# Unscaled scores on VectorE and the inverse root in the exponentials of ScalarE, for the last four narrow jobs

## The chip, the cores and the metric

The kernel runs on one core of a Trainium2 chip. The metric is the device time of one execution in microseconds, lower is better. Before the change the median of three runs was 381.04 us (380.89 to 381.19).

## The reference

Four cross-attention layers run one after another on `x` (8 batches x 128 tokens x 128 channels) against a context of 8 x 128 x 256. Layers 0 and 3 are narrow: 16 query heads of width 8 over 4 key/value heads, with an RMS norm of the input. Layers 1 and 2 are wide: 16 heads of width 64 and a bias on a few key columns. Cut to what matters:

```python
def narrow(x, cond, wq, wk, wv, wo, norm_w):                  # layers 0 and 3
    inv = rsqrt(mean(x * x, axis=-1) + 1e-5)                  # one number per token
    q = (x * inv * norm_w) @ wq;  k = cond @ wk;  v = cond @ wv
    scores = einsum('btgrd,bsgd->bgrts', q, k) / sqrt(8)
    attn = softmax(scores)                                    # over the 128 keys
    return x + einsum('bgrts,bsgd->btgrd', attn, v) @ wo
def wide(x, cond, Wq, Wk, Wv, Wo, bo):                        # layers 1 and 2
    return softmax(q @ k.T / 8 + col_bias) @ v @ Wo + bo + x
x = narrow(wide(wide(narrow(x, L0), L1), L2), L3)
```

The inverse root `inv` is one factor per token (per row of scores), so it may be applied to the scores in place of the input.

## The kernel before, in words

A job is one layer for one batch, 32 jobs in all. They are ordered in two turns of 16: the first turn does all four layers for batches 0 to 3, the second for batches 4 to 7. The last four jobs, n = 28 to 31, are therefore layer 3, narrow, for batches 4 to 7. A job has two halves, o = 2n and 2n + 1, and a half has two sides; one side is a score tile of 128 tokens x 512 (four heads x 128 keys), in one PSUM bank. The last four jobs are halves 56 to 63.

The order of work on every engine is written out by hand in that engine's `half` function, and every engine takes its instructions strictly in that order, with semaphores between engines. Nothing is planned at run time. A side goes through these steps:

- TensorE, `scores` (L825 narrow, L836 wide): the scores, with sign reversed by the factor put on the queries.
- VectorE, `scores_out` (L615): four instructions of 128x128, one for each head. Each copies negated scores from PSUM to `probs`, adds a bias (`no_bias`, a column of zeros that is broadcast, in narrow jobs), multiplies by `scale`, and accumulates the minimum over keys to `negmax`. In narrow jobs `scale` is the per-token column `inv_rms`, read from memory; in wide jobs it is the constant 1.0. A short read of the accumulator follows each.
- ScalarE, `exponentials` (L482): four activations of 128x128, exp(-1.0 * e + negmax), in place, each with its row sum and a read of the accumulator. The scale is a constant and the bias a column.
- VectorE, `inverse_sums` (L622): reciprocal of the row sums. GpSimd, `normalise` (L379): multiplies probabilities by it.
- TensorE, `transpose_probs` (L849), two halves later. The transposed tile is copied out (`probsT`) by VectorE for side 0 (L626) and, in halves whose own job is narrow, by ScalarE for side 1 (L499). That copy stands between the exponentials of side 0 and side 1 of the half two later.
- TensorE, weighted values (L870 narrow, L882 wide), VectorE `oT` (L631, L633), TensorE output projection (L900), VectorE adds the input (L641, L643), and a DMA stores the batch after layer 3 (L310).

VectorE's order within half o is: add the input of job n - 2 and write the mean square (L586) if o is odd; `scores_out(o, 0)`; `inverse_sums(o - 1, 1)`; `scores_out(o, 1)`; `oT`; if o is even, the two instructions that make the next job's queries (L594, L598); copies of the transposes of half o - 2; `inverse_sums(o, 0)`. ScalarE's order in the last halves is: exponentials of side 0, the copy L499, exponentials of side 1.

The inverse root of job n is made by GpSimd (`inverse_root`, L361) in its half 2n - 2, from the mean that VectorE wrote; VectorE waits for it before the first scores of the job.

Of the kernel before, what the change touches and what calls it, by code (L numbers as in the profile page):

```python
# [27 lines left out]
ALU = mybir.AluOpType  # L28
ACT = mybir.ActivationFunctionType
# [4 lines left out]
P = 128  # L34
# [15 lines left out]
NARROW = (0, 3)  # L50
# [23 lines left out]
NJOBS = len(JOBS)  # L74
NARROW_JOBS = [n for n, (l, b) in enumerate(JOBS) if l in NARROW]
WIDE_ROWS = [(p, l) for p, l in ROWS if l not in NARROW]
NARROW_ROWS = [(p, l) for p, l in ROWS if l in NARROW]
KV_RING = 3
KD_RING = 2
# [33 lines left out]
def job(n):  # L113

    return JOBS[n] if 0 <= n < NJOBS else (None, None)
# [12 lines left out]
def uses(n, h):  # L128

    return sum(2 if is_wide(m) else 1 for m in range(n)) + (h + 1 if is_wide(n) else 1)  # L130


def scores_bank(o):

    return "fill" if o >= LAST_FILL + 2 and o % 2 == 1 else "scores"
# [12 lines left out]
def narrow_index(n):  # L148

    return NARROW_JOBS.index(n)  # L150


def build(nc, xT, ctxT, narrow_w, narrow_kv, kv_w, qo_w, small, tokens, outT):
    with ExitStack() as ctx:
        def sb(name, shape, dt=F32):
            return ctx.enter_context(nc.sbuf_tensor(name, shape, dt))

        def sem(name):
            return ctx.enter_context(nc.semaphore(name))
# [38 lines left out]
        x_sq = sb("x_sq", [P, 2, T])  # L198
        rms = sb("rms", [P, 2])
        inv_rms = sb("inv_rms", [P, 2])  # L200
        c_hi = sb("c_hi", [P, PAIRS, CC, PAIR], F32R)
        c_lo = sb("c_lo", [P, PAIRS, CC, PAIR], F32R)
        kT = sb("kT", [P, KV_RING, IC, PAIR])
# [13 lines left out]
        negmax = sb("negmax", [P, 2, 2, 4])  # L217
# [32 lines left out]
        sq_ready, rms_out, rms_made = sem("sq_ready"), sem("rms_out"), sem("rms_made")  # L250
# [6 lines left out]
        pt_full, pt_read = pair("pt_full"), pair("pt_read")  # L257
        v_full, v_read = sem("v_full"), sem("v_read")
        y_full, y_read = sem("y_full"), sem("y_read")
        out_stored = sem("out_stored")  # L260

        HALVES = [(n, h) for n in range(NJOBS + 2) for h in range(2)]
# [51 lines left out]
        def _(pool):  # L314
# [43 lines left out]
            def inverse_root(n):  # L358

                pool.wait_ge(rms_out, narrow_index(n) + 1)  # L360
                nc.gpsimd.tensor_tensor(inv_rms[:, n % 2:n % 2 + 1], rms[:, n % 2:n % 2 + 1], half_power[:],  # L361
                                        ALU.pow).then_inc(rms_made, 1)

            def square(n):

                l, b = job(n)
                if l == 0:
                    pool.wait_ge(x_loaded[0 if b < 2 else 1], 16)
                else:
                    pool.wait_ge(y_read, JOBS.index((2, b)) + 1)  # L370
                if narrow_index(n) >= 2:
                    pool.wait_ge(ms_full, narrow_index(n) - 1)
                nc.gpsimd.tensor_tensor(x_sq[:, n % 2, :], x[:, b, :], x[:, b, :], ALU.mult).then_inc(sq_ready, 1)
# [19 lines left out]
            def half(o):  # L393
                if valid(o):
                    normalise(o, 0)
                    normalise(o, 1)
                for n in NARROW_JOBS:
                    if o == 2 * n - 2 and n > 0:
                        inverse_root(n)
                    if o == 2 * n - 4 and n >= 2:  # L400
                        square(n)
                    if o == keys_half(n):
                        if job(n)[1] % 2 == 0:
                            split_keys(f"kn{job(n)[1] // 2}.{job(n)[0]}")
                        diagonal_keys(n)
                    if o == 2 * n:
                        narrow_values(n)
                if o in (3, 4):
                    split_piece(o + 1)
                if o == 9:  # L410
                    split_context(2)
                if o == 10:
                    split_context(3)
# [6 lines left out]
            pool.wait_ge(smalls_loaded, 16)  # L420
            diagonal_keys(0)
            inverse_root(0)
            square(1)
            diagonal_keys(1)
# [5 lines left out]
        def _(act):  # L430
# [46 lines left out]
            def exponentials(o, side):  # L477

                act.wait_ge(scores_read[side], o + 1)
                for q in range(4):  # L480
                    e = probs[:, o % PROBS_RING, side, q * S:(q + 1) * S]
                    last = nc.scalar.activation(e, e, ACT.Exp, scale=-1.0, bias=negmax[:, o % 2, side, q:q + 1],  # L482
                                                accum_out=rowsum[:, o % 2, side, q:q + 1])
                last.then_inc(exps_made[side], 1)

            def half(n, h):
                o = 2 * n + h
                if h == 0 and is_wide(n):
                    wide_queries(n, 1)
                if h == 1 and is_wide(n + 1):  # L490
                    wide_queries(n + 1, 0)
                for name in FILLS.get(o - 1, [])[1:]:
                    if name != "bias":
                        fill_out(name)
                if valid(o):
                    exponentials(o, 0)
                if scalar_copy(o - 2):
                    act.wait_ge(pt_full[1], o - 1)
                    nc.scalar.activation(probsT[:, (o - 2) % PROBST_RING, 1, :], pt_ps[1][:], ACT.Copy).then_inc(pt_read[1], 1)  # L499
                if valid(o):  # L500
                    exponentials(o, 1)
                for name in FILLS.get(o, [])[:1]:
                    fill_out(name)
                if o in (0, 1):
                    round_piece(o + 2)
                if 3 <= o <= 6:
                    round_piece(o + 1)
# [18 lines left out]
        def _(dve):  # L526
# [77 lines left out]
            def scores_out(o, side):  # L604

                n, h = o // 2, o % 2
                l, b = job(n)
                bias = no_bias[:].broadcast_to([P, S]) if l in NARROW else col_bias[:, l - 1, :]
                scale = inv_rms[:, n % 2:n % 2 + 1] if l in NARROW else 1.0
                if l in NARROW and h == 0 and side == 0:  # L610
                    dve.wait_ge(rms_made, narrow_index(n) + 1)
                dve.wait_ge(scores_full[side], o + 1)
                for q in range(4):
                    cols = slice(q * S, (q + 1) * S)
                    last = nc.vector.tensor_tensor_reduce(  # L615
                        out=probs[:, o % PROBS_RING, side, cols], in0=banks[scores_bank(o)][side][:, cols], in1=bias, scale=scale,
                        scalar=HUGE, op0=ALU.add, op1=ALU.min, accum_out=negmax[:, o % 2, side, q:q + 1])
                last.then_inc(scores_read[side], 1)
# [28 lines left out]
            def half(n, h):  # L647
# [5 lines left out]
                if valid(o):  # L653
                    scores_out(o, 0)
                if valid(o - 1):
                    inverse_sums(o - 1, 1)
                if valid(o):
                    scores_out(o, 1)
# [38 lines left out]
        def _(pe):  # L697
# [14 lines left out]
            def context_split(p):  # L712
                if p == 0:
                    pe.wait_ge(c_split, 1)
                else:
                    pe.wait_ge(rest_split, p)
# [7 lines left out]
            def project_context(name):  # L724
# [29 lines left out]
                else:  # L754
                    f, m = int(name[1]), int(name[3])
                    p, l = WIDE_ROWS[f]
                    context_split(p)
# [51 lines left out]
            def scores(n, h):  # L809
# [18 lines left out]
                pe.wait_ge(q_read, uses(n, h))  # L828
                f = WIDE_ROWS.index((b // 2, l))
                for m in (2 * h, 2 * h + 1):  # L830
# [21 lines left out]
            def weighted_values(n, h):  # L852
# [12 lines left out]
                if l in NARROW:  # L865
# [9 lines left out]
                    return  # L875
                f = WIDE_ROWS.index((b // 2, l))
                name = f"v{f}.{2 * (b % 2) + h}"
# [123 lines left out]
```

## Time and profile before

| | us |
|---|---|
| median of three runs | 381.04 |
| the profiled execution, its own time | 380.89 |
| its span (first to last instruction) | 379.1 |
| outside the span | 1.79 |
| busy PE / DVE / ACT / POOL | 359.7 / 267.7 / 279.0 / 187.6 |

Half 56 starts on VectorE at 333.98 us, the last exponential ends at 371.46 us, and the span ends at 379.1 us. Each half can be found by its first exponential of ScalarE, at 335.19 us for half 56, 341.28 for 57, 345.37 for 58, 351.01 for 59, 354.58 for 60 and 359.87 for 61. PE is TensorE's matmuls, PEld its weight loads, DVE VectorE, ACT ScalarE, POOL GpSimd, SP the engine that issues the stores. Busy time overlaps a little between neighbouring instructions of one engine, because each starts before the last has quite ended: a mean duration is not always the distance from start to start.

### The profile page before, as it was taken

To read this page: it belongs to the slowest core of one execution; us is meant where nothing else is said; L and a number is where in the kernel's file an instruction comes from. 1 tells how busy PE (TensorE), PEld (TensorE's weight loads), DVE (VectorE), ACT (ScalarE), POOL (GpSimd) and SP (SyncE) were. 2 spreads that over 40 slices of the span, in tenths; PEclk is the share of its full clock that TensorE was granted. 3 is DMA by queue.
4 is the path that set the end of the run, shared out by engine and by line. 5 is a ranking of instruction groups with operands and counts; after the bars stand their busy time and mean duration, and the time that the engine had idled before them with its cause. 6 is when DMAs were issued, how large, how long until landed. Compare 5 with 4: busy or idle time off the path is not lost.

```text
span 379.1 us, 10494 instructions
## 1 busy us (share of the span) xinstructions
PE 359.7 (95%) x3522; PEld 319.1 (84%) x3522; DVE 267.7 (71%) x1401; ACT 279.0 (74%) x1176; POOL 187.6 (49%) x220
## 2 busy tenths in 40 slices
PE   8889999999999999999999999999999999978665
PEld 8787799899999998889889988888999989867554
DVE  2999975636536547696978886577564785699982
ACT  4889998865665567475899999998566865647793
POOL 3677853733223236454676765443333435447662
PEclk9899999999999999999999999999999999999979
DMA  7925000000000000000000000000000000000000
GB/s 232 411 66 216 1 3 3 2 3 2 1 2 3 2 0 3 2 3 0 10 3 9 9 8 2 3 3 2 0 3 2 3 2 1 2 3 3 7 9 14
DMA packets 4883, 9.91 MB, mean 26 GB/s; under 512 B 608, under 2 KB 3296, under 8 KB 4576
## 3 DMA queue, kind: packets, MB, share of 16 engines
q1 hardware_dynamic: 4400, 8.91, 6.5%
q8 instruction: 29, 0.48, 0.5%
q10 hardware_dynamic: 432, 0.34, 0.4%
q14 instruction: 22, 0.18, 0.2%
HBM read 8.73 MB, written 0.52 MB: 24 GB/s over the span
## 4 chain that ended last, share of the span: by engine, by line
PE 74%; DVE 21%; ACT 3%; issue 1%; DVEq 0%; POOL 0%; POOLq 0%
PE pt_ps L849 13%; PE scores_ps L836 9%; DVE probs L615 8%; PE q_ps L796 8%; PE fill_ps L701 7%; PE v_ps L900 7%; PE v_ps L882 7%; PE fill_ps L702 7%; PE fill_ps L703 7%; PE v_ps L870 3%; DVE probsT L626 3%; ACT probs L482 3%; PE q_ps L788 2%; DVE qn L598 2%; DVE qn L594 2%; PE scores_ps L825 2%
## 5 line engine op out<-in xcount | busy, mean ns | idle before, releaser
L482 ACT ACTIVATE probs<-probs,negmax 128x128 f32<-128x128 f32 x512 | 198.5, 391 | 81.0 <-DVE negmax L615 80.9
L379 POOL TENSOR_TENSOR probs<-probs,inv 128x512 f32<-128x512 f32 x128 | 137.3, 1075 | 176.8 <-DVE inv L622 176.4
L482 ACT ACTIVATION_READ_ACCUMULATOR probs<-probs,negmax 128x1 f32 x512 | 96.8, 189 | 0.0
L615 DVE CUSTOM_DVE_ANT_0 probs<-scores_ps,col_bias 128x128 f32<-128x128 f32 x256 | 58.2, 284 | 39.1 <-PE scores_ps L836 39.1
L849 PE MATMUL pt_ps<-smalls,probs 128*128 128x128 f32 x512 | 70.5, 282 | 6.2 <-DVE probsT L626 6.2
L849 PEld LDWEIGHTS pt_ps<-smalls,probs 128*128 128x128 f32 x512 | 57.6, 143 | 18.2 <-issue 14.8
L615 DVE CUSTOM_DVE_ANT_0 probs<-scores_ps,no_bias,inv_rms 128x128 f32<-128x128 f32 x224 | 64.2, 343 | 5.8 <-PE scores_ps L825 5.4
L626 DVE COPY probsT<-pt_ps 128x512 f32<-128x512 f32 x96 | 63.0, 684 | 2.6 <-PE pt_ps L849 0.5
L615 DVE DVE_READ_ACCUMULATOR2_ANT negmax<- 128x1 f32 x512 | 42.5, 83 | 0.0
L701 PE MATMUL fill_ps<-c_hi,w_hi 128*128 128x256 f32 x128 | 38.3, 300 | 0.0
L836 PE MATMUL scores_ps<-kT,qT 64*128 64x128 f32 x512 | 37.2, 285 | 0.0
L882 PE MATMUL v_ps<-probsT,v 128*64 128x128 f32 x512 | 35.0, 279 | 1.6 <-DVE rms L586 1.0
L702 PE MATMUL fill_ps<-c_hi,w_lo 128*128 128x256 f32 x128 | 36.1, 282 | 0.0
L703 PE MATMUL fill_ps<-c_lo,w_hi 128*128 128x256 f32 x128 | 36.0, 281 | 0.0
L836 PEld LDWEIGHTS scores_ps<-kT,qT 64*128 64x128 f32 x512 | 31.1, 187 | 3.9
L796 PE MATMUL q_ps<-x,w_qo 128*128 128x128 f32 x256 | 34.0, 276 | 0.0
L882 PEld LDWEIGHTS v_ps<-probsT,v 128*64 128x64 f32 x512 | 27.4, 136 | 7.1 <-issue 4.0
L796 PEld LDWEIGHTS q_ps<-x,w_qo 128*128 128x128 f32 x256 | 31.9, 191 | 1.3 <-issue 0.4
L900 PE MATMUL v_ps<-oT,w_qo 128*128 128x128 f32 x256 | 31.7, 277 | 0.0
L643 DVE SCALAR_TENSOR_TENSOR x<-v_ps,smalls,x 128x128 f32<-128x128 f32 x16 | 5.6, 347 | 35.3 <-PE v_ps L900 35.3
L900 PEld LDWEIGHTS v_ps<-oT,w_qo 128*128 128x128 f32 x256 | 29.9, 192 | 0.0
L701 PE MATMUL fill_ps<-w_hi,c_hi 128*128 128x512 f32 x64 | 27.5, 430 | 0.3 <-ACT v L468 0.3
(92 smaller groups left out, 583.2 us busy)
## 6 DMA issues: line engine op xcount, KB each, us to landing
kT<-in_kv_w SPq DMA_DIRECT2D x6, 512.0 KB, 6.4
w_qo<-in_qo_w SPq DMA_DIRECT2D x2, 1024.0 KB, 8.3
v<-in_ctxT SPq DMA_DIRECT2D x4, 256.0 KB, 9.5
v<-in_kv_w SPq DMA_DIRECT2D x2, 512.0 KB, 11.2
outT<-x SPq DMA_DIRECT2D x8, 64.0 KB, 1.6
wn<-in_narrow_w SPq DMA_DIRECT2D x2, 192.0 KB, 5.7
x<-in_xT SPq DMA_DIRECT2D x1, 384.0 KB, 8.1
oT<-in_narrow_kv ACTq DMA_DIRECT2D x1, 256.0 KB, 3.9
```

The costliest lines, as they stand in the source:

```text
L379: nc.gpsimd.tensor_tensor(p4, p4, inv[:, o % 2, side, :].unsqueeze(2).broadcast_to([P, 4, S]), ALU.mult,).then_inc(probs_made[side], 1)
L482: last = nc.scalar.activation(e, e, ACT.Exp, scale=-1.0, bias=negmax[:, o % 2, side, q:q + 1], accum_out=rowsum[:, o % 2, side, q:q + 1])
L615: last = nc.vector.tensor_tensor_reduce(out=probs[:, o % PROBS_RING, side, cols], in0=banks[scores_bank(o)][side][:, cols], in1=bias, scal ...
L626: nc.vector.tensor_copy(probsT[:, o % PROBST_RING, side, :], pt_ps[side][:]).then_inc(pt_read[side], 1)
L701: nc.tensor.matmul(out, a_hi, b_hi, start=(n == 0), stop=False)
L702: nc.tensor.matmul(out, a_lo, b_hi, start=False, stop=False)
L703: last = nc.tensor.matmul(out, a_hi, b_lo, start=False, stop=(n == len(moving) - 1))
L796: last = nc.tensor.matmul(q_ps[:, c * T:(c + 1) * T], w_qo[:, l - 1, first:first + P], x[:, b, :], start=True, stop=True)
L836: last = nc.tensor.matmul(out[side][:, c * S:(c + 1) * S], qT[rows, 4 * h + c, :], kT[rows, f % KV_RING, 4 * h + c, b % 2 * S:(b % 2 + 1) ...
L849: last = nc.tensor.transpose(pt_ps[side][:, cols], probs[:, o % PROBS_RING, side, cols], identity)
L882: last = nc.tensor.matmul(v_ps[side * WIDE_D:(side + 1) * WIDE_D, c * T:(c + 1) * T], v[:, f % KV_RING, b % 2, head * WIDE_D:(head + 1) * ...
L900: last = nc.tensor.matmul(y_ps, w, oT[:, c, :], start=(c == 0), stop=(c == (1 if l in NARROW else IC) - 1))
```

## The change

In jobs 28 to 31 (`n >= LATE`) VectorE no longer multiplies the scores by `inv_rms`. Its `scale` is the constant 1.0, as in wide jobs, it still adds the broadcast column of zeros, and it no longer waits for the inverse root. ScalarE makes `shift = inv_rms * negmax` (an activation of 128x4, one per side) and then takes exp(neg_rms * e + shift), with `neg_rms` and `shift` as columns. ScalarE waits for its own write of `shift` and for `neg_rms`, which GpSimd makes by one more instruction of 128x1 for each job, right behind the inverse root and after a wait for it.

```diff
--- before.py
+++ after.py
@@ -74,6 +74,8 @@
 NJOBS = len(JOBS)
 NARROW_JOBS = [n for n, (l, b) in enumerate(JOBS) if l in NARROW]
 WIDE_ROWS = [(p, l) for p, l in ROWS if l not in NARROW]
+
+LATE = NJOBS - 4
 NARROW_ROWS = [(p, l) for p, l in ROWS if l in NARROW]
 KV_RING = 3
 KD_RING = 2
@@ -198,6 +200,8 @@
         x_sq = sb("x_sq", [P, 2, T])
         rms = sb("rms", [P, 2])
         inv_rms = sb("inv_rms", [P, 2])
+        neg_rms = sb("neg_rms", [P, 2])
+        shift = sb("shift", [P, 2, 2, 4])
         c_hi = sb("c_hi", [P, PAIRS, CC, PAIR], F32R)
         c_lo = sb("c_lo", [P, PAIRS, CC, PAIR], F32R)
         kT = sb("kT", [P, KV_RING, IC, PAIR])
@@ -257,6 +261,7 @@
         pt_full, pt_read = pair("pt_full"), pair("pt_read")
         v_full, v_read = sem("v_full"), sem("v_read")
         y_full, y_read = sem("y_full"), sem("y_read")
+        neg_made, shift_made = sem("neg_made"), sem("shift_made")
         out_stored = sem("out_stored")
 
         HALVES = [(n, h) for n in range(NJOBS + 2) for h in range(2)]
@@ -360,6 +365,10 @@
                 pool.wait_ge(rms_out, narrow_index(n) + 1)
                 nc.gpsimd.tensor_tensor(inv_rms[:, n % 2:n % 2 + 1], rms[:, n % 2:n % 2 + 1], half_power[:],
                                         ALU.pow).then_inc(rms_made, 1)
+                if n >= LATE:
+                    pool.wait_ge(rms_made, narrow_index(n) + 1)
+                    nc.gpsimd.tensor_scalar(neg_rms[:, n % 2:n % 2 + 1], inv_rms[:, n % 2:n % 2 + 1], -1.0, None,
+                                            ALU.mult).then_inc(neg_made, 1)
 
             def square(n):
 
@@ -477,9 +486,17 @@
             def exponentials(o, side):
 
                 act.wait_ge(scores_read[side], o + 1)
+                n = o // 2
+                offset, scale = negmax, -1.0
+                if n >= LATE:
+                    act.wait_ge(neg_made, n - LATE + 1)
+                    nc.scalar.activation(shift[:, o % 2, side, :], negmax[:, o % 2, side, :], ACT.Copy,
+                                         scale=inv_rms[:, n % 2:n % 2 + 1]).then_inc(shift_made, 1)
+                    act.wait_ge(shift_made, 2 * (o - 2 * LATE) + side + 1)
+                    offset, scale = shift, neg_rms[:, n % 2:n % 2 + 1]
                 for q in range(4):
                     e = probs[:, o % PROBS_RING, side, q * S:(q + 1) * S]
-                    last = nc.scalar.activation(e, e, ACT.Exp, scale=-1.0, bias=negmax[:, o % 2, side, q:q + 1],
+                    last = nc.scalar.activation(e, e, ACT.Exp, scale=scale, bias=offset[:, o % 2, side, q:q + 1],
                                                 accum_out=rowsum[:, o % 2, side, q:q + 1])
                 last.then_inc(exps_made[side], 1)
 
@@ -606,8 +623,9 @@
                 n, h = o // 2, o % 2
                 l, b = job(n)
                 bias = no_bias[:].broadcast_to([P, S]) if l in NARROW else col_bias[:, l - 1, :]
-                scale = inv_rms[:, n % 2:n % 2 + 1] if l in NARROW else 1.0
-                if l in NARROW and h == 0 and side == 0:
+                normalised = l in NARROW and n < LATE
+                scale = inv_rms[:, n % 2:n % 2 + 1] if normalised else 1.0
+                if normalised and h == 0 and side == 0:
                     dve.wait_ge(rms_made, narrow_index(n) + 1)
                 dve.wait_ge(scores_full[side], o + 1)
                 for q in range(4):
```

## Rows read from the trace of the kernel before

**Rows 1.** The page, busy time and share of the span of each engine, whole kernel.
```profile
PE 359.7 (95%) x3522; PEld 319.1 (84%) x3522; DVE 267.7 (71%) x1401; ACT 279.0 (74%) x1176; POOL 187.6 (49%) x220
```

**Rows 2.** Windows view, three stretches: start:end, length, busy of PE, PEld, DVE, ACT, POOL, granted clock.
```profile
349.80:358.70 8.90, 5.79 (x67) 4.57 (x66) 8.02 (x46) 7.23 (x34) 5.93 (x9) 0.98 0.01 3
...
358.70:366.60 7.90, 6.99 (x54) 5.39 (x54) 6.56 (x42) 6.73 (x32) 4.78 (x7) 0.59 0.03 8
...
366.60:379.10 12.50, 6.25 (x93) 4.77 (x92) 5.67 (x27) 5.24 (x23) 4.24 (x5) 0.99 0.06 17
```

**Rows 3.** Waits view of ScalarE and VectorE from 338 us: total us, times, longest.
```profile
ACT probs L482 <- DVE negmax L615: 8.1, 5, 2.9
...
DVE inv L622 <- ACT probs L482: 3.2, 3, 1.8
```

**Rows 4.** Groups by form, VectorE, whole kernel: line, shapes, count, busy us, mean ns.
```profile
L615 DVE CUSTOM_DVE_ANT_0 probs<-scores_ps,no_bias,inv_rms 128x128 f32<-128x128 f32 x224 | 64.2, 343 | 5.8 <-PE scores_ps L825 5.4 <-DVE col_bias L562 0.4
...
L615 DVE CUSTOM_DVE_ANT_0 probs<-scores_ps,col_bias 128x128 f32<-128x128 f32 x256 | 58.2, 284 | 39.1 <-PE scores_ps L836 39.1
...
L643 DVE SCALAR_TENSOR_TENSOR x<-v_ps,smalls,x 128x128 f32<-128x128 f32 x16 | 5.6, 347 | 35.3 <-PE v_ps L900 35.3
...
L641 DVE TENSOR_TENSOR x<-v_ps,x 128x128 f32<-128x128 f32 x16 | 4.5, 284 | 9.0 <-PE v_ps L900 9.0
```

**Rows 5.** Groups by form, ScalarE, whole kernel, same columns.
```profile
L482 ACT ACTIVATE probs<-probs,negmax 128x128 f32<-128x128 f32 x512 | 198.5, 391 | 81.0 <-DVE negmax L615 80.9
...
L434 ACT ACTIVATE w_hi<-kT 128x1024 fp32r<-128x1024 f32 x6 | 6.3, 1050 | 1.4 <-DMA kT<-in_kv_w 1.4
...
L516 ACT ACTIVATE c_hi<-v 128x512 fp32r<-128x512 f32 x1 | 0.6, 612 | 0.0
```

**Rows 6.** Groups by form, GpSimd: the inverse root.
```profile
L361 POOL TENSOR_TENSOR inv_rms<-rms,half_power 128x1 f32<-128x1 f32 x16 | 8.9, 554 | 0.0
```

**Rows 7.** Timeline, halves 56 to 58: start, length, engine, line, what, idle before it.
```profile
335.19 0.40 ACT L482 ACTIVATE probs<-probs,negmax 128x128 f32<-128x128 f32 x1 [1.94 <-DVE negmax L615]
...
336.82 0.68 DVE L594 TENSOR_SCALAR qn<-q_ps 96x512 fp32r<-96x512 f32 x1
...
337.54 0.68 DVE L598 SCALAR_TENSOR_TENSOR qn<-q_ps,qn 32x512 fp32r<-32x512 f32 x1
...
341.28 0.41 ACT L482 ACTIVATE probs<-probs,negmax 128x128 f32<-128x128 f32 x1 [2.91 <-DVE negmax L615]
...
345.26 0.17 DVE L622 RECIPROCAL inv<-rowsum 128x4 f32<-128x4 f32 x1
```

**Rows 8.** Timeline, halves 59 to 61, ScalarE and VectorE.
```profile
351.01 0.40 ACT L482 ACTIVATE probs<-probs,negmax 128x128 f32<-128x128 f32 x1 [1.97 <-DVE negmax L615]
...
352.57 0.57 ACT L499 ACTIVATE probsT<-pt_ps 128x512 f32<-128x512 f32 x1
...
354.58 0.39 ACT L482 ACTIVATE probs<-probs,negmax 128x128 f32<-128x128 f32 x1
...
354.71 0.18 DVE L622 RECIPROCAL inv<-rowsum 128x4 f32<-128x4 f32 x1 [0.66 <-ACT probs L482]
...
359.87 0.40 ACT L482 ACTIVATE probs<-probs,negmax 128x128 f32<-128x128 f32 x1 [1.63 <-DVE negmax L615]
```

**Rows 9.** Timeline, TensorE from 358 us, transposes and weighted values.
```profile
358.45 1.94 PE L849 MATMUL pt_ps<-smalls,probs 128*128 128x128 f32 x8 [1.03 <-DVE probsT L626]
...
363.60 1.79 PE L870 MATMUL v_ps<-probsT,v_narrow 128*32 128x128 f32 x32
...
369.66 1.06 PE L849 MATMUL pt_ps<-smalls,probs 128*128 128x128 f32 x8 [2.00 <-DVE probsT L626]
...
374.79 1.08 PE L870 MATMUL v_ps<-probsT,v_narrow 128*32 128x128 f32 x32 [0.89 <-ACT probsT L499]
```

**Rows 10.** Timeline, after the last exponentials, VectorE and GpSimd.
```profile
371.50 0.18 DVE L622 RECIPROCAL inv<-rowsum 128x4 f32<-128x4 f32 x1 [1.84 <-ACT probs L482]
...
371.75 1.04 POOL L379 TENSOR_TENSOR probs<-probs,inv 128x512 f32<-128x512 f32 x1 [0.98 <-DVE inv L622]
```

## Prediction

> **What bounds the kernel now.** I read the page first, then the windows over the last 30 us, then the waits of the two engines that the change touches. Over the whole kernel TensorE is the busy engine, 95% of the span [rows 1], but that is no guide to the last four jobs: there TensorE's busy time is 5.79 us in a stretch of 8.90, and in the next stretch 6.99 of 7.90 only because the granted clock was 0.59, that is mostly 1.2 GHz in place of 2.4 [rows 2]. In these stretches VectorE is busy 8.02 of 8.90 and 6.56 of 7.90, ScalarE 7.23 and 6.73. So neither has much room, and they take turns. The waits show it from both sides [rows 3]: the exponentials waited for VectorE's scores 5 times, 8.1 us in all, and VectorE's reciprocal waited for the exponentials 3 times, 3.2 us. The question is therefore not what VectorE saves but how far ScalarE can grow before it sets the pace alone.
>
> The timeline gives each engine's pace. In ScalarE the exponentials of half 59 begin at 351.01, the copy at 352.57, and half 60 follows at 354.58 without a gap: a half with a copy is a block of 3.57 us, eight exponentials of 0.39 from start to start (3.12) and 0.45 for the copy. VectorE's reciprocal of half 59, side 1, starts at 354.71, 0.13 after the block's end, and waited 0.66 for it; the second score tile of half 60 is queued behind that reciprocal [rows 8]. From this reciprocal to the exponentials of half 61 (359.87) it is 5.16 us. In half 61 ScalarE waited 1.63 for VectorE.
>
> **VectorE: what goes.** In halves 56 to 63 there are 64 score instructions. With the column `inv_rms` as scale one takes 343 ns, with the constant 1.0 in wide jobs 284 [rows 4]: 59 ns each, 0.47 us per half, 3.8 us in all. The wide form reads a bias of 128x128 and the narrow form a broadcast column, so the difference could belong to the bias. Against that stand the additions of the input: with a column as scalar 347 ns, without 284, same shape [rows 4]. Bounds: 0 and 63 ns; I take 59. The wait for the inverse root goes too; no wait of that kind is among VectorE's [rows 3], so it is worth nothing.
>
> **ScalarE: what comes.** Two things.
>
> First, each exponential gets a second column, the scale. No row shows an activation with two. The nearest rows: with one column (the bias) an exponential of 128x128 takes 391 ns. Activations with constants alone take 1050 ns for 1024 columns and 612 for 512 [rows 5], so 0.855 ns for a column, and one of 128 would take 612 - 384 x 0.855 = 284. The first column operand thus costs up to 107 ns (the row sum may have part of it). For the second the bounds are 0, if it is read beside the first, and 107. I take 100, 0.80 us per half, because VectorE's case [rows 4] shows such a read to be a cost in itself.
> The Trainium skill (ScalarE: Activation LUTs, section "What ACT_TABLE_LOAD costs") speaks against this change: each `[128,1]` pointer operand adds about 93 ns to an activation. The trace agrees for the first one (391 against its 280 + 0.833 x 128 = 387); for the second no row exists. By it the term would be 0.74 per half; if the second read were hidden it would be 0.
>
> Second, two `shift` activations per half. At 4 columns the same line through rows 5 gives 612 - 508 x 0.855 = 178 ns, with a column as scale up to 285; the next instruction waits for its write. VectorE has such a wait for its own result: L594 ends at 337.50, L598 starts at 337.54, 0.04 later [rows 7]. I take 0.28 + 0.04 = 0.32 per side, 0.64 per half. Bounds: 0.18 (no second column cost, no gap) and 0.42. What is queued behind it: that side's exponentials, behind these the copy of the transposes, and VectorE, which waits with the next score tile behind its reciprocal.
>
> A block grows by 0.80 + 0.64 = 1.44: to 5.01 us with the copy, and 3.12 + 1.44 = 4.56 without (half 57).
>
> **GpSimd.** Four more instructions of 128x1, at most the 554 ns of the inverse root itself [rows 6], with a wait for it. GpSimd is busy 5.93 of 8.90 and 4.78 of 7.90 us [rows 2], and ScalarE needs `neg_rms` only two halves later. I count nothing; without that cover it would be 0.55 per job on the normalisation queued behind, 1.1 us for two jobs near the end. The column of zeros is read as before.
>
> **The sum, along the chain.** Half 56: ScalarE starts 0.24 early and takes 4.56, from 335.19 to about 339.5, while VectorE has not yet reached the scores of half 57. No loss.
> Half 57: VectorE was never held in these two halves, so its start comes with the savings of 12 instructions, 0.71 early: 341.28 - 0.71 = 340.57 [rows 7]. ScalarE ends at 340.57 + 4.56 = 345.13; VectorE's reciprocal comes at 345.26, the very time of before [rows 7]. VectorE's lead of 1.2 us is gone.
> Half 59: from that reciprocal to the start of half 59 it was 351.01 - 345.26 = 5.75 [rows 7, 8]; less the 8 instructions of a half (0.47) 5.28. So 350.54. ScalarE's own block 58 ends at 345.13 + 5.01 = 350.14: it waits for VectorE here for the last time.
> Halves 59 to 63: from a reciprocal to the next start VectorE needs 5.16 - 0.47 = 4.69 in the half that makes queries [rows 8], less than 5.01, and less in the odd ones. ScalarE now runs through: 350.54 + 5 x 5.01 = 375.59, and the last reciprocal at 375.72 against 371.50 [rows 10]. That is 4.2 us later, of which the lead of 0.47 at half 59 is already taken off. Of the 3.8 us saved on VectorE no more than that 0.47 reaches the end.
>
> From there the last normalisation (GpSimd, 371.75, 1.04 us [rows 10]), transposes, copy, weighted values, projection and store follow each other with nothing changed, so the end moves with it: +4.2.
>
> **TensorE's clock in the end.** More waiting opens between TensorE's bursts. Before, the clock fell to 1.2 GHz after pauses of 1 to 2 us (the transposes of 358.45, after one of 1.03, took 1.94 us), but held through one of 2.00 (369.66, 1.06 us) [rows 9]. In the new order the transposes of half 62 wait for a copy 2.7 us into ScalarE's last block, so the pause ahead of them is near 4 us. At the low clock the last transposes take 1.94 instead of 1.06 and the weighted values 1.79 instead of 1.08 [rows 9], 1.6 us on the path, and some 0.4 for what lies around them. Bounds 0 and 2.0; I take the middle, 1.0, as the clock can recover between the two.
>
> Sum: +4.2 + 1.0 = +5.2. The profiled execution took 380.89 (span 379.1), so 386.1; the median lies 0.15 above it: **386.2 us**.
>
> **The rivals.**
> - *The second column costs nothing in the exponentials.* The block is then 3.57 + 0.64 = 4.21. Half 57 starts at 340.57, ends at 344.33; half 59 starts at 344.46 + 5.28 = 349.74; half 60 at 353.95; half 61 is held by VectorE, 354.08 + 4.69 = 358.77; then 362.98, 367.19, end 371.40, reciprocal 371.53. That is no change, 381.1. For it: both columns might be read together. Against: each is a separate operand, and the first has its price in rows 5.
> - *Faster: VectorE's saving reaches the end.* It needs the second column free and the shift at its lower bound (0.18) or hidden. With no growth at all half 59 starts at 351.01 - 24 x 0.059 = 349.6, half 60 at 353.2, half 61 at 353.3 + 4.69 = 358.0, 1.9 us early, and the end likewise: 379.1. With shifts of 0.18 I get about -0.8, 380.2. It decides as long as a block stays below some 4.1 us. For it: ScalarE waited 8.1 us for scores [rows 3]. Against: those waits are mostly in halves 56 and 57, and half 60 had none.
> - *VectorE saves nothing* (the 59 ns belonged to the bias). Half 57 starts at 341.28, half 58 at 345.84, half 59 at 345.97 + 5.75 = 351.72, half 60 at 356.73, half 61 is held by VectorE, 356.86 + 5.16 = 362.02; three blocks bring 377.05, 1.5 us later still: 387.7. Against: the additions in rows 4.
> - *As forecast, with the clock at one of its ends*: 385.2 (full speed) or 387.2 (low).
>
> **How the numbers follow.** Forecast, with either clock, 0.76; second column free 0.10; faster 0.07; VectorE saves nothing 0.07. The range of 383.2 to 388.2 takes in a second column at about half price with the clock at full speed on one side (block 4.6, about +2.2), and on the other shifts of 0.42 or nothing saved on VectorE with the low clock. What a measurement can tell from no change is about 0.2%, 0.8 us. Faster 0.08 (the third case and a part of the second), the same 0.06, slower 0.86.
>
> **What would show it.** The scores of jobs 28 to 31 at 284 ns in VectorE; the exponentials of halves 56 to 63 near 490 ns, and 0.48 from start to start; shifts of 0.28 us, 0.32 ahead of the first exponential; ScalarE without a wait from half 59 to 63, and a wait of VectorE's reciprocal in every half; a distance of 5.0 us between halves. If exponentials stay at 391, the forecast is wrong at its main term. If ScalarE still waits for scores in halves 61 and 63, VectorE or TensorE is the pace, and the chain above is wrong. If the last transposes take 1.06 us, the clock's term goes.

## The result and the profile after

The changed kernel takes 385.67 us (median of 4 runs, 385.23 to 386.13), the kernel before 380.97 (380.52 to 381.19). The ratio is 1.0113, 95% interval 1.0082 to 1.0145. The profiled execution took 385.48 with a span of 383.7, 4.6 more than before.

The page of the changed kernel, busy time of the engines:

```profile
PE 359.4 (94%) x3522; PEld 317.4 (83%) x3522; DVE 263.8 (69%) x1401; ACT 289.4 (75%) x1192; POOL 189.2 (49%) x224
```

VectorE has lost 3.9 us and ScalarE has gained 10.4 [rows 1]. The groups by form, from 333 us on (line, shapes, count, busy us, mean ns), give the prices:

```profile
L633 DVE CUSTOM_DVE_ANT_0 probs<-fill_ps,no_bias 128x128 f32<-128x128 f32 x32 | 7.2, 281 | 0.0
...
L499 ACT ACTIVATE probs<-probs,shift,neg_rms 128x128 f32<-128x128 f32 x64 | 30.8, 482 | 0.5
...
L493 ACT ACTIVATE shift<-negmax,inv_rms 128x4 f32<-128x4 f32 x16 | 4.6, 286 | 3.0 <-DVE negmax L633 3.0
...
L370 POOL TENSOR_SCALAR neg_rms<-inv_rms 128x1 f32<-128x1 f32 x3 | 0.7, 224 | 0.3
```

A score instruction takes 281 ns with the constant (32 of the 64; the other 32 take 278), though it still reads the broadcast column of zeros: the 59 ns of [rows 4] belong to the scale column. An exponential with two columns takes 482 ns, 91 more than with one [rows 5]. A shift takes 286 ns. GpSimd's added instruction takes 224.

The waits from 338 us (total, times, longest), which answer to [rows 3]:

```profile
ACT shift L493 <- DVE negmax L633: 1.4, 2, 1.0
...
DVE inv L640 <- ACT probs L499: 11.5, 10, 2.5
```

They are turned round. ScalarE waits for scores 1.4 us in place of 8.1, and VectorE's reciprocal waits for exponentials 10 times, 11.5 us, in place of 3 times, 3.2. The timeline of ScalarE, the first shift of halves 57 to 61, and the last reciprocal with what follows it, which answer to [rows 7, 8, 10]:

```profile
340.71 0.30 ACT L493 ACTIVATE shift<-negmax,inv_rms 128x4 f32<-128x4 f32 x1 [1.02 <-DVE negmax L633]
...
345.21 0.28 ACT L493 ACTIVATE shift<-negmax,inv_rms 128x4 f32<-128x4 f32 x1
...
350.61 0.30 ACT L493 ACTIVATE shift<-negmax,inv_rms 128x4 f32<-128x4 f32 x1 [0.34 <-DVE negmax L633]
...
355.58 0.28 ACT L493 ACTIVATE shift<-negmax,inv_rms 128x4 f32<-128x4 f32 x1
...
360.55 0.28 ACT L493 ACTIVATE shift<-negmax,inv_rms 128x4 f32<-128x4 f32 x1
...
375.56 0.18 DVE L640 RECIPROCAL inv<-rowsum 128x4 f32<-128x4 f32 x1 [2.54 <-ACT probs L499]
...
375.82 1.04 POOL L388 TENSOR_TENSOR probs<-probs,inv 128x512 f32<-128x512 f32 x1 [1.68 <-DVE inv L640]
```

The short wait at half 59 (0.34) is the last for scores: 350.61, 355.58 and 360.55 lie 4.97 apart. TensorE's timeline at the end, against [rows 9]:

```profile
373.43 1.03 PE L867 MATMUL pt_ps<-smalls,probs 128*128 128x128 f32 x4 [0.46 <-ACT probsT L516]
...
374.40 1.94 PE L888 MATMUL v_ps<-probsT,v_narrow 128*32 128x128 f32 x32
...
377.43 1.06 PE L867 MATMUL pt_ps<-smalls,probs 128*128 128x128 f32 x8
```

Three stretches of the windows view (columns as in [rows 2], the granted clock is the third number from the right):

```profile
370.00:372.00 2.00, 0.00 (x0) 0.00 (x0) 1.40 (x10) 1.97 (x9) 1.14 (x2) 1.00 0.02 4
...
374.00:376.00 2.00, 2.00 (x35) 1.45 (x33) 0.18 (x1) 2.00 (x9) 0.32 (x2) 0.50 0.03 8
...
376.00:378.00 2.00, 1.46 (x15) 0.96 (x8) 1.18 (x3) 0.01 (x1) 0.86 (x1) 0.77 0.00 0
```

TensorE did nothing from 370 to 372, its clock was at 1.2 GHz (0.50) from 374 to 376, and the weighted values of half 61 took 1.94 us. The last transposes ran at full clock again (1.06), but 1.87 us after the last reciprocal instead of 1.34, because TensorE was behind with the slow weighted values and the projection that follows them.

### The profile page after: what moved, and what is told of

It is laid out like the page before. It is cut to its first block, busy times and chain, and to the rows that moved or that the text cites. A ratio compares the mean times of both kernels' runs of the same rounds, so it can differ in the third digit from the quotient of the medians.

```text
span 383.7 us, 10526 instructions
## 1 busy us (share of the span) xinstructions
PE 359.4 (94%) x3522; PEld 317.4 (83%) x3522; DVE 263.8 (69%) x1401; ACT 289.4 (75%) x1192; POOL 189.2 (49%) x224
## 4 chain that ended last, share of the span: by engine, by line
PE 73%; DVE 15%; ACT 7%; issue 2%; DMA 1%; DVEq 0%
PE pt_ps L867 12%; PE scores_ps L854 9%; PE v_ps L918 8%; PE q_ps L814 8%; PE v_ps L900 8%; PE fill_ps L719 7%; PE fill_ps L720 7%; PE fill_ps L721 7%; DVE probs L633 6%; ACT probs L499 6%; PE v_ps L888 3%; PE q_ps L806 2%; DVE probsT L644 2%; PE scores_ps L843 2%; DVE qn L615 2%
## 5 line engine op out<-in xcount | busy, mean ns | idle before, releaser
L499 ACT ACTIVATE probs<-probs,negmax 128x128 f32<-128x128 f32 x448 | 173.8, 392 | 71.4 <-DVE negmax L633 71.3
L499 ACT ACTIVATION_READ_ACCUMULATOR probs<-probs,negmax 128x1 f32 x448 | 85.1, 190 | 0.0
L633 DVE CUSTOM_DVE_ANT_0 probs<-scores_ps,no_bias,inv_rms 128x128 f32<-128x128 f32 x192 | 55.0, 343 | 5.9 <-PE scores_ps L843 5.5
L640 DVE RECIPROCAL inv<-rowsum 128x4 f32<-128x4 f32 x128 | 22.2, 173 | 14.6 <-ACT probs L499 13.9
L499 ACT ACTIVATE probs<-probs,shift,neg_rms 128x128 f32<-128x128 f32 x64 | 30.8, 482 | 0.5
```

The source lines that it names most:

```text
L499: last = nc.scalar.activation(e, e, ACT.Exp, scale=scale, bias=offset[:, o % 2, side, q:q + 1], accum_out=rowsum[:, o % 2, side, q:q + 1])
L633: last = nc.vector.tensor_tensor_reduce(out=probs[:, o % PROBS_RING, side, cols], in0=banks[scores_bank(o)][side][:, cols], in1=bias, scal ...
```

## The experiments

Each kernel ran beside the kernel before on the same chip. A profile gives four numbers that add up to its span, and by these most runs are read, since the whole times scatter by up to 5 us: where the last halves start (first exponential or shift of half 56, against 335.19, or 334.95 where VectorE's first scores are unscaled), the chain (the last reciprocal, less that shift of the start, against 371.50), from the last reciprocal to the last transposes (1.34 before), and from there to the end (6.26 before). Each kernel has one profile, so the four numbers are those of one execution, and only the last two columns stand for all runs.

| kernel | span | start | chain | to transposes | to the end | runs, median us | ratio (95%) |
|---|---|---|---|---|---|---|---|
| changed | 383.7 | +0.16 | +3.90 | +0.53 | 0 | 385.67 | 1.0113 (1.0082-1.0145) |
| e1_column | 380.9 | -0.08 | +2.13 | -0.24 | 0 | 385.33 | 1.0094 (1.0063-1.0125) |
| e2_shift | 383.3 | -0.95 | +1.81 | +1.34 | +2.0 | 384.44 | 1.0077 (1.0050-1.0103) |
| e5_both | 385.3 | +0.31 | +5.43 | +0.50 | 0 | 387.24 | 1.0160 (1.0134-1.0187) |
| e3_vector | 377.1 | -0.32 | -2.99 | +1.36 | 0 | 378.78 | 0.9927 (0.9902-0.9952) |
| e4_busy | 389.4 | -0.04 | +5.26 | +5.12 | 0 | 389.64 | 1.0233 (1.0208-1.0259) |
| e12_busy12 | 382.8 | +0.01 | +3.90 | -0.24 | 0 | 384.33 | 1.0067 (1.0044-1.0089) |
| e13_column_busy10 | 382.1 | -0.09 | +2.14 | -0.24 | +1.2 | 384.33 | 1.0069 (1.0044-1.0094) |
| e7_first_job | 379.9 | -0.86 | -0.04 | +1.72 | 0 | 383.29 | 1.0037 (1.0007-1.0068) |
| e6_chosen | 378.1 | -0.02 | -0.99 | 0 | 0 | 380.36 | 0.9997 (0.9980-1.0015) |
| e9_column_busy | 387.4 | +0.54 | +3.99 | +3.77 | 0 | 389.39 | 1.0221 (1.0202-1.0239) |
| e10_chosen_busy | 384.2 | -0.23 | +1.39 | +3.95 | 0 | 386.14 | 1.0135 (1.0113-1.0156) |
| e14_chosen_busy8 | 379.9 | +2.11 | -1.34 | 0 | 0 | 380.60 | 0.9973 (0.9949-0.9996) |

My theory: the change makes ScalarE the engine that sets the pace. It gets 1.40 us more per half, where VectorE gives up 0.47, and what comes through is what exceeds the slack. Rivals: the added work on ScalarE is all on the path, or hidden; or VectorE's saving comes through.

**The column alone (e1_column).**

```diff
+            nc.gpsimd.memset(minus_one[:], -1.0)
...
-  activation(e, e, ACT.Exp, scale=-1.0, bias=negmax[...])
+  scale = minus_one[:] if o >= 2 * NJOBS - 8 else -1.0
+  activation(e, e, ACT.Exp, scale=scale, bias=negmax[...])
```

> The kernel before, but in halves 56 to 63 the exponentials take their scale of -1.0 from a column instead of a constant; VectorE scales as before, there is no shift. My chain: an exponential goes from 391 to 482 ns, a half of ScalarE from 3.57 to 4.30 us; half 60 starts 0.7 later, half 61 1.0, each later one 0.7 to 0.4, and the last reciprocal comes at 373.7 instead of 371.5: +2.2 us, 383.2 (up to 0.5 more if TensorE's clock falls in the last half). Rival 1, all of it is on the path: 64 x 0.091 = +5.8, 386.8. Rival 2, it is hidden in the 8.1 us that ScalarE waited for scores: 381.0.

Timeline of this kernel: the start of half 61 and the last reciprocal.

```profile
360.52 0.49 ACT L485 ACTIVATE probs<-probs,negmax,minus_one 128x128 f32<-128x128 f32 x1 [0.89 <-DVE negmax L618]
...
373.55 0.18 DVE L625 RECIPROCAL inv<-rowsum 128x4 f32<-128x4 f32 x1 [2.21 <-ACT probs L485]
```

The chain is +2.13 where +2.2 was expected, with the last wait of ScalarE at half 61; neither the 5.8 nor the 0 of the rivals. This reading rests on the profiled run, the shortest of six (382.71). The five others took 384.71 to 385.77, and the median is 4.1 us above the kernel before, which this chain doesn't explain. On record for each run is TensorE's mean granted clock: 0.990 in the profiled one, 0.966 to 0.973 in the five others (below, the clock).

**The shift alone (e2_shift).**

```diff
                 act.wait_ge(scores_read[side], o + 1)
+                if o >= 2 * NJOBS - 8:
+                    nc.scalar.activation(shift[...], negmax[...], ACT.Copy, scale=inv_rms[...]).then_inc(shift_made, 1)
+                    act.wait_ge(shift_made, 2 * (o - 2 * NJOBS + 8) + side + 1)
```

> The kernel before, with the shift activations of 128x4 and ScalarE's wait for each added in halves 56 to 63, but their result unused: VectorE scales and the exponentials keep their constant. My chain: a half grows by 0.64 to 4.2 us, the last reciprocal comes at 373.4: +1.9 us, 382.9. Rival 1, all on the path: 16 x 0.32 = +5.1, 386.1. Rival 2, hidden: 381.0. With the column alone and this alone I expect 2.2 + 1.9 = 4.1 in two kernels, less than the two together cost on an unchanged VectorE.

From its timeline the start of half 56, the last reciprocal and the last transposes, and then two stretches of its windows:

```profile
334.24 0.30 ACT L483 ACTIVATE shift<-negmax,inv_rms 128x4 f32<-128x4 f32 x1 [1.94 <-DVE negmax L621]
...
372.36 0.18 DVE L628 RECIPROCAL inv<-rowsum 128x4 f32<-128x4 f32 x1 [2.17 <-ACT probs L488]
...
375.04 1.94 PE L855 MATMUL pt_ps<-smalls,probs 128*128 128x128 f32 x8
```

```profile
364.00:370.00 6.00, 4.03 (x28) 2.86 (x17) 5.36 (x31) 5.90 (x29) 3.27 (x4) 0.50 0.04 11
...
376.00:382.00 6.00, 3.71 (x39) 2.59 (x37) 1.27 (x3) 0.60 (x1) 0.00 (x0) 0.50 0.04 11
```

The chain is +1.81, expected +1.9. The whole time (385.33; the median is 384.44, expected 382.9) is more, and the rows say where: in this run the last transposes took 1.94 us, and TensorE's clock was at 1.2 GHz (0.50) in both windows; 1.34 us were lost before the transposes and 2.0 behind.

**ScalarE's half of the change on the old VectorE (e5_both).** Both edits above.

> ScalarE's half of the change without VectorE's: the column as scale (-1.0) and the shift activations (result unused) in halves 56 to 63, VectorE scales as before. My chain with blocks of 4.97 us: half 57 at 341.28, half 59 at 351.7, half 61 held by VectorE at 361.9, last reciprocal near 377.0: +5.5, with 0.5 for TensorE's clock in the last half 387.0 us, 1.3 above the changed kernel. So VectorE's 3.8 us are worth about 1.3 to 1.5 there. Rival: ScalarE alone sets the pace from half 57 on, VectorE's saving is worth nothing: 385.7.

From its timeline the start of half 56 and the last reciprocal:

```profile
335.50 0.30 ACT L485 ACTIVATE shift<-negmax,inv_rms 128x4 f32<-128x4 f32 x1 [1.94 <-DVE negmax L624]
...
377.24 0.18 DVE L631 RECIPROCAL inv<-rowsum 128x4 f32<-128x4 f32 x1 [2.54 <-ACT probs L491]
```

The chain is +5.43, against 2.13 + 1.81 = 3.94 for the two apart, and the median 387.24, expected 387.0. The slack is used once: what each edit found free alone, the two must share. The changed kernel's chain is 1.53 shorter. That is all that VectorE's 3.8 us bring once ScalarE is burdened.

**VectorE's half alone (e3_vector).** The inverse root is left out of jobs 28 to 31.

```diff
-                scale = inv_rms[...] if l in NARROW else 1.0
+                scaled = l in NARROW and n < NJOBS - 4
+                scale = inv_rms[...] if scaled else 1.0
```

> VectorE's half of the change alone: in jobs 28 to 31 the scores are not scaled, ScalarE is as before. The inverse root is left out of these jobs. It shows what VectorE's saving is worth where ScalarE pays nothing. My chain: half 59 starts 1.4 early, half 61 1.9 early, the end likewise: 379.1 us. Rival: the saving of 3.8 us is all on the path: 377.2; or TensorE's pace in halves 61 to 63 holds it: within 0.5 of 381.0.

From its timeline the starts of halves 57, 59 and 61, weighted values, the last reciprocal and the last transposes:

```profile
340.24 0.40 ACT L482 ACTIVATE probs<-probs,negmax 128x128 f32<-128x128 f32 x1 [2.42 <-DVE negmax L616]
...
349.00 0.40 ACT L482 ACTIVATE probs<-probs,negmax 128x128 f32<-128x128 f32 x1 [1.48 <-DVE negmax L616]
...
357.37 0.40 ACT L482 ACTIVATE probs<-probs,negmax 128x128 f32<-128x128 f32 x1 [1.15 <-DVE negmax L616]
...
360.46 1.08 PE L871 MATMUL v_ps<-probsT,v_narrow 128*32 128x128 f32 x32
...
368.19 0.18 DVE L623 RECIPROCAL inv<-rowsum 128x4 f32<-128x4 f32 x1 [1.84 <-ACT probs L482]
...
370.89 1.06 PE L850 MATMUL pt_ps<-smalls,probs 128*128 128x128 f32 x8 [0.20 <-DVE probsT L627]
```

378.78 was measured where 379.1 was expected, but two errors met. The chain gained 2.99 us, not 1.9: half 59 came 1.69 early (28 shorter instructions lead up to it; I had counted 24), half 61 2.18, and 0.8 more was won up to the last reciprocal: the weighted values before half 63 ran at full clock this time (1.08 us, 1.79 before), and VectorE had no wait for them, where it had waited 0.67 us before. Then the clock fell (0.70 granted from 366 to 368 us, 0.50 from 368 to 370), and the last transposes came 2.70 us after the reciprocal instead of 1.34.

**Where ScalarE has room (e7_first_job, e6_chosen).** A list `PLAIN` of (half, side) says which sides take the new form.

```diff
-                if n >= LATE:
+                if (o, side) in PLAIN:           # on ScalarE
-                normalised = l in NARROW and n < LATE
+                normalised = l in NARROW and (o, side) not in PLAIN   # on VectorE
# e7_first_job:  PLAIN = both sides of halves 56, 57
# e6_chosen:     PLAIN = (56,0) (56,1) (57,0) (58,0) (58,1) (60,1)
```

> The new form in job 28 alone (halves 56 and 57). My chain: half 57 starts 0.7 early, ScalarE's block of 4.5 us eats it, and VectorE's next reciprocal comes at 345.2 instead of 345.26: no difference, 380.9, with ScalarE 3 us busier than before in these halves. Rival 1: each us on ScalarE costs, +2.7. Rival 2: VectorE's 0.94 us come through: 380.0.

Timeline of e7_first_job, the start of half 56, the reciprocal behind half 57, the start of half 59, the last reciprocal and the last transposes:

```profile
334.09 0.30 ACT L494 ACTIVATE shift<-negmax,inv_rms 128x4 f32<-128x4 f32 x1 [1.61 <-DVE negmax L634]
...
344.32 0.18 DVE L641 RECIPROCAL inv<-rowsum 128x4 f32<-128x4 f32 x1 [0.73 <-ACT probs L500]
...
350.16 0.40 ACT L500 ACTIVATE probs<-probs,negmax 128x128 f32<-128x128 f32 x1 [2.31 <-DVE negmax L634]
...
370.60 0.18 DVE L641 RECIPROCAL inv<-rowsum 128x4 f32<-128x4 f32 x1 [1.84 <-ACT probs L500]
...
373.66 1.06 PE L868 MATMUL pt_ps<-smalls,probs 128*128 128x128 f32 x8 [0.20 <-DVE probsT L645]
```

The start is 0.86 early in this run. With that added the reciprocal behind half 57 is at 345.18, half 59 at 351.02 and the last reciprocal at 371.46: against [rows 7, 8, 10] nothing has moved. VectorE's 0.94 us and ScalarE's 2.7 us (16 x 0.091 + 4 x 0.32) cancel within the slack, as expected. The whole time was not as expected: 12 runs from 380.75 to 385.90, median 383.29. In the profiled one the granted clock was 0.50 from 364 to 372 us, and the last transposes came 3.06 us after the reciprocal, 1.72 more than before. The mean granted clock goes with the time here too: 0.986 to 0.991 in the four runs up to 381.72, 0.971 to 0.981 in the eight from 383.06 up.

> The same choice of sides without the added matmuls. My chain: 379.6 with full clock in the last half; if the longer pauses lower it, up to 2 us more in some runs. The difference to the run before shows what the clock does to a kernel whose chain is otherwise the same.

Timeline of e6_chosen, the starts of halves 59, 61 and 63 and the last reciprocal:

```profile
350.01 0.40 ACT L500 ACTIVATE probs<-probs,negmax 128x128 f32<-128x128 f32 x1 [0.54 <-DVE negmax L634]
...
358.62 0.40 ACT L500 ACTIVATE probs<-probs,negmax 128x128 f32<-128x128 f32 x1 [0.69 <-DVE negmax L634]
...
366.79 0.40 ACT L500 ACTIVATE probs<-probs,negmax 128x128 f32<-128x128 f32 x1 [0.93 <-DVE negmax L634]
...
370.49 0.18 DVE L641 RECIPROCAL inv<-rowsum 128x4 f32<-128x4 f32 x1 [1.84 <-ACT probs L500]
```

Halves 59 and 61 start 0.98 and 1.23 early (1.18 and 1.4 expected), counted from the start of half 56, and the chain ends 0.99 early, where 1.4 was expected. Nine of 12 runs took 379.97 to 380.50 (mean granted clock 0.986 to 0.995), three 381.90 to 383.20 (0.977 to 0.982); by its interval this kernel is no different from the one before.

**The clock at the end (e4_busy, e9_column_busy, e10_chosen_busy).** Matmuls of no use in TensorE's pauses.

```diff
+                if 62 <= o <= 63: busy(6)      # after the scores
+                if 61 <= o <= 63: busy(8)      # after the weighted values
+                if o == 63: busy(24)           # e9: 16, e10: 14
+   busy: nc.tensor.matmul(q_ps[:, 0:T], mean_w[:], mean_w[:], start=True, stop=True)
```

> The changed kernel with matmuls of no use added on TensorE where it pauses (8 in half 61, 14 in half 62, 38 in half 63, into the bank of the queries, which is free by then), so that its clock stays up in the last half. Theory: some of the changed kernel's runs end with a low clock, which costs 0.5 us in the profiled one; with the clock held the last transposes start 1.35 us after the last reciprocal, and the time is 385.0 with runs close together. Rival: the clock in the end is of no account, 385.7 as before; or the added matmuls hold up the transposes: over 386.

> The column of -1.0 alone (as in the run e1_column) with the same kind of matmuls in TensorE's pauses (8, 14 and 30). There the profiled run, with full clock in its last half, took 382.7, while five others took 384.7 to 385.8. Theory: those five ended at the low clock, which is worth 2 to 3 us; with it held all runs come to 382.7 to 383.2, 2.2 above before. Rival: the profiled run was the exception for another reason, and the median stays at 385.3.

> The new form only where VectorE sets the pace and ScalarE waits: halves 56 and 58, side 0 of half 57, side 1 of half 60; the old form elsewhere; matmuls in TensorE's pauses as above (8, 14, 28). My chain: half 59 starts 1.18 early, half 61 1.4 early, the end likewise: 379.6 at most, less by up to 0.5 if the clock gives something. Rival: ScalarE's growth is on the path wherever it is made: 24 x 0.091 + 6 x 0.32 = 4.1 later, 385.

Timeline of e4_busy, the added matmuls at the end of half 63 and the last transposes, and a stretch of its windows:

```profile
372.89 7.31 PE L953 MATMUL q_ps<-mean_w 128*128 128x128 f32 x64
...
383.18 1.06 PE L867 MATMUL pt_ps<-smalls,probs 128*128 128x128 f32 x8 [0.20 <-DVE probsT L644]
```

```profile
374.00:376.00 2.00, 2.00 (x20) 2.00 (x19) 0.18 (x1) 1.97 (x7) 1.04 (x1) 1.00 0.01 4
```

All three failed on their size. The trace shows each of these matmuls as two records, so the 64 from 372.89 on are the last 32 of the 38 in half 63. They lasted 7.31 us, 0.23 each, where I had reckoned with 0.13 as for a transpose. The clock held (1.00), but TensorE was the bound: medians of 389.64, 389.39 and 386.14 us. The expectations of the next runs use 0.192 each, which is 7.31 divided by 38 and too low. Fewer of them, in one pause:

```diff
+                if o == 63:                    # e13: 10, e14: 8
+                    for _ in range(12):
+                        nc.tensor.matmul(q_ps[:, 0:T], mean_w[:], mean_w[:], start=True, stop=True)
```

> The changed kernel with 12 matmuls of no use in the one pause of TensorE at the end of half 63 (3.25 us in the profile; 12 x 0.192 = 2.3 us, so they don't reach the next transposes; in e4_busy the added ones filled the engine and were the bound). Theory: the clock no longer falls at 373.7, the last transposes follow the last reciprocal by 1.35 us and the time is 385.0 to 385.2. Rival: the clock falls all the same, or costs nothing there: 385.7.

Its added matmuls, last reciprocal and last transposes, from the timeline:

```profile
369.89 3.55 PE L946 MATMUL q_ps<-mean_w 128*128 128x128 f32 x24
...
375.41 0.18 DVE L640 RECIPROCAL inv<-rowsum 128x4 f32<-128x4 f32 x1 [2.54 <-ACT probs L499]
...
376.51 1.07 PE L867 MATMUL pt_ps<-smalls,probs 128*128 128x128 f32 x8 [0.20 <-DVE probsT L644]
```

Chain +3.90, exactly that of the changed kernel, and the last transposes 1.10 us after the reciprocal instead of 1.87. All 11 runs lie between 383.53 and 384.80, median 384.33, below every run of the changed kernel and below the 385.0 to 385.2 expected. If that is all the clock, its share in the median of the changed kernel is some 1.3 us, more than the 0.53 of its profiled run. That isn't shown: the two were not run side by side, and the intervals of their ratios to the kernel before overlap. Nor did the clock simply hold. In this profiled run it was at 1.2 GHz (0.50) from 364 to 371 us and at full speed from 372 to 380, so it rose while the added matmuls ran. At the low clock these lasted 3.55 us, not 2.3, and reached up to the next transposes; the path didn't suffer. Whether they raised the clock or it would have risen without them, one profile can't tell.

> The column of -1.0 alone, with 10 such matmuls (1.9 us) at the end of half 63, where TensorE paused 2.8 us in the profile. Theory: the runs of e1_column at 384.7 to 385.8 ended at the low clock, and with this pause filled the median comes to 382.7 to 383.2. Rival: the clock had fallen before this pause in those runs, or something else made them long: the median stays near 385.3.

Its added matmuls, last transposes and last weighted values, from the timeline:

```profile
368.27 2.40 PE L931 MATMUL q_ps<-mean_w 128*128 128x128 f32 x20
...
374.65 1.07 PE L852 MATMUL pt_ps<-smalls,probs 128*128 128x128 f32 x8 [0.20 <-DVE probsT L629]
...
376.60 1.94 PE L873 MATMUL v_ps<-probsT,v_narrow 128*32 128x128 f32 x32 [0.88 <-ACT probsT L502]
```

Half right. Six of 12 runs came to 382.68 to 383.89, where one of six had been before, the rest stayed at 384.76 to 385.43. The profiled run (383.89) shows that filling one pause is no hold: the clock fell behind the last transposes (1.07 us), and the weighted values took 1.94. The other runs have no profile, but their mean granted clock divides them: 0.982 to 0.990 in the six short ones, 0.971 to 0.977 in the six long. That bears out the clock as what goes with the long runs. It doesn't show where in them it was low, nor that it alone made them long.

> The chosen sides (halves 56 and 58, side 0 of 57, side 1 of 60) with 8 matmuls (1.5 us) at the end of half 63. e6_chosen had its profiled run at 379.97, 0.9 below the profiled run before, but 3 of 12 runs at 381.9 to 383.2. Theory: these are falls of the clock in the last half; with the pause filled all runs come to 380.0 to 380.4, and the median is 0.7 below before. Rival: the scatter stays, the median is that of before.

Its start of half 56, last reciprocal and last transposes, from the timeline:

```profile
337.06 0.30 ACT L494 ACTIVATE shift<-negmax,inv_rms 128x4 f32<-128x4 f32 x1 [1.61 <-DVE negmax L634]
...
372.27 0.18 DVE L641 RECIPROCAL inv<-rowsum 128x4 f32<-128x4 f32 x1 [1.84 <-ACT probs L500]
...
373.61 1.06 PE L868 MATMUL pt_ps<-smalls,probs 128*128 128x128 f32 x8 [0.20 <-DVE probsT L645]
```

Chain -1.34, and a ratio of 0.9973 (0.9949 to 0.9996): the one version with the whole computation whose interval lies below 1, by a quarter of a percent and only just; e6_chosen, the same without the added matmuls, doesn't. The theory of the scatter fails here: 12 runs from 379.36 to 382.11, and the mean granted clock doesn't order them (0.986 at 379.77 and at 381.89). The profiled one (381.74) was not long in its end. Its last halves began 2.11 us late, at 337.06, ahead of everything that this study changes.

The traces show where this lateness begins. VectorE's first instruction that splits the context, in the kernel before, in e7_first_job and here:

```profile
10.10 1.39 DVE L692 TENSOR_TENSOR c_lo<-v,c_hi 128x512 fp32r<-128x512 f32 x1
...
9.61 0.72 DVE L711 TENSOR_TENSOR c_lo<-v,c_hi 128x512 fp32r<-128x512 f32 x1
...
10.44 2.62 DVE L711 TENSOR_TENSOR c_lo<-v,c_hi 128x512 fp32r<-128x512 f32 x1
```

The same instruction lasted 1.39, 0.72 and 2.62 us, and the first reciprocal followed at 14.83, 13.67 and 16.41. Of the 2.11 us, 1.58 are there within the first 17 us. Over all profiles it lasted about 0.7 where the last halves began 0.9 early (e2_shift, e7_first_job) and 1.2 to 1.5 where they began within 0.6 of the time before. So there are two sources of scatter. The second lies mostly in the start of the kernel, and why this instruction varies stays open.

## Why the prediction was right

- **VectorE's saving**, 59 ns each, 0.47 per half: held (281 against 284). The broadcast column was not the cause.
- **The second column**, 100 ns, bounds 0 and 107: 91. This was the term that decided. The Trainium skill, ScalarE: Activation LUTs, section "What ACT_TABLE_LOAD costs", has about 93 ns for each pointer operand; the trace agrees for the second (482 less 391).
- **The shift**, 0.28 + 0.04: 0.286 + 0.03.
- **The block**, 5.01 us: 4.97. **The steps of the chain**, halves 57, 58 and 59 at 340.57, 345.13, 350.54, last reciprocal at 375.72: measured 340.71, 345.21, 350.61 and 375.56, with 0.16 of it a later start. +4.2 was forecast, +3.90 is the chain's own (+4.06 with the start).
- **GpSimd** at nothing: held. ScalarE's wait for `neg_rms` appears nowhere.
- **The clock**, 1.0 between 0 and 2.0: too large for the profiled run (0.53); for the median it may be some 1.3, by e12_busy12, which isn't shown. I had put it at the last transposes; it fell one step earlier, on those of half 62 and the weighted values of half 61, and had recovered before the last ones. The pause ahead was 3.25 us, not near 4. My sign for it was wrong too: the last transposes did take 1.06 us, and yet 0.53 was lost. That the sum comes so near is in this term partly luck. It was the middle between wide bounds, and what it stands for is -0.24 to 3.3 us in the profiled runs of the table whose added matmuls weren't themselves the bound.
- **The rivals.** That the second column is free fell with 482 ns. The faster one was right in its mechanism (e3_vector, 378.78) but its condition, that ScalarE doesn't grow, isn't met. The argument against it was misread: of the 8.1 us that ScalarE waited for scores, 2.91 were in half 57 and 5.2 in halves 58, 59, 61 and 63, so not mostly in halves 56 and 57. "VectorE saves nothing" was priced at 387.7; e5_both, which is that case, took 387.24.

Against the profiled execution the forecast was 386.1 to 385.48: 0.15 of the difference is the chain with its start, the rest the clock.

## What to carry to other kernels

Moving a factor from one engine to another that is used in turns with it is paid in that engine's own price for the operand: here 59 ns left VectorE and 91 came to ScalarE, plus a small instruction with a wait for itself that cost 0.32 us each for 4 columns. Where two engines alternate, work out the block of each and the slack at each hand-over; a saving counts only in the halves where its engine is the later one, and there the same change on chosen sides shortened the chain by 1.0 to 1.3 us (e6_chosen, e14_chosen_busy8), where the whole of it lengthened it by 3.9. Two edits that each fit half into the slack don't fit together (2.13 and 1.81 apart, 5.43 together).

## What the runs showed of the hardware

- The time of this kernel, whose engines pause in the last 20 us, depends in part on when TensorE's clock falls. With the chain unmoved (e7_first_job) 1.72 us were lost in the profiled run, at a granted clock of 0.50 from 364 to 372 us, and 12 runs spread over 5.2 us; the kernel before, in 34 runs beside it, over 3.6 (380.20 to 383.78). In e1_column, e6_chosen, e7_first_job and e13_column_busy10 every run of the long group has a lower mean granted clock than every run of the short one; in e14_chosen_busy8 there is no such order.
- One VectorE instruction of 128x512 in the first 14 us lasted from 0.69 (e2_shift) to 2.62 us (e14_chosen_busy8) in the profiles, and the last halves began early or late with it (0.95 early, 2.11 late).
- Small uneven additions to a kernel can so cost more through the clock than through their own time: e2_shift lost 1.81 in the chain and 3.3 to the clock in its profiled run.
- With one pause filled by 12 matmuls of no use the median of the changed kernel came out 1.3 us lower (e12_busy12, not side by side), and in e13_column_busy10 half of the runs were short instead of one in six. Ten of these matmuls took 2.40 us at full clock, 0.24 each; eight transposes of the same size take 1.06, 0.13 each.
